# A's transposes in a fused cross-attention kernel: sixteen on VectorE, or four on TensorE

## The chip, the core and the metric

One core of a Trainium2 chip runs the whole program. The time is the device time of one execution in microseconds, the median of several runs. Its engines work side by side, each through its own list of instructions, and meet at semaphores: PE is TensorE (matmuls; PEld are its weight loads), DVE is VectorE, ACT is ScalarE, POOL is GpSimd, SP is SyncE, whose queue issues the DMAs.

## What is computed

```python
x: (16, 256, 1024)   ctx: (16, 256, 512)   W_mem: (1024, 512)   W_gate: (1024, 2048)

P      = einsum('bme,de->bmd', ctx, W_mem)          # memory_proj
S      = einsum('bnd,bmd->bnm', x, P) / sqrt(1024)
A      = softmax(S, axis=-1)
C      = einsum('bnm,bmd->bnd', A, P)               # memory_context
gate   = sigmoid(concat([x, C], -1) @ W_gate.T + b_gate)
fused  = x + gate * C
out    = fused * rsqrt(mean(fused**2, -1) + 1e-6) * norm_w
```

Everything is float32. The kernel keeps that precision with products of the type fp32r: each operand is split into a high part (a ScalarE copy that rounds) and a low part (a subtraction), and each product is made of three, high x high, high x low and low x high.

## The kernel before, in words

It works through 16 batches, one after the other: batch 0 and batch 15 are written out, batches 1 to 14 are a loop on every engine. Before batch 0 the weights are loaded, turned and split; the half of W_gate that belongs to C is multiplied with W_mem once into K, so that the gate's second half can be made from ctx: C @ G2.T = (A @ ctx) @ K.

TensorE's order within a batch, by `batch` in the tensor block:
- P from the turned ctx (`ct_h`, `ct_l`) and `wt`: 48 products of 512 columns
- the gate's X block of the second 128 rows, `gate_x(1, ...)`: 48 products of 512 columns
- the gate's X block of the first 128 rows, `gate_x(0, 0, before_s)`: the first 2 of 8 k (3 in batch 0), 6 products each
- the scores, 48 products of 256 columns, into `psum[:, 6:8, 0:M]`, the first halves of banks 6 and 7 (`s_mm`)
- the rest of the first X block, `gate_x(0, before_s, KD)`, line 803, into banks 0 and 1 (`xt_used`)
- TT, the turned A @ ctx: 24 products of 256 columns into banks 6 and 7, after the waits for `cn_ready` and `at_ready` (line 807)
- the memory products A @ P (the second after a wait for `tt_ready`), then the gate's second half.

Between scores and TT runs the softmax: DVE takes the row maxima from the score banks (line 607) and negates them (609), ACT makes `prob` in SBUF with the exponential and its row sum (450), DVE takes the reciprocal (611) and scales `prob` with it in two instructions (614, `prob_ready`). Then A has to be turned, because TT and the memory products contract over its columns: `turn_a` (lines 560 to 567) writes `at32` in SBUF with 16 VectorE transposes of 32x32 blocks and raises `at_turned`. ACT copies `at32` to `at_h` (line 457; in the trace line 400, the helper `copy`), DVE subtracts to `at_l` (line 619; in the trace line 505, the helper `low`) and raises `at_ready`. In ACT's list the copy of ctx, `ctt_h`, stands between the exponential and `at_h`. Behind `at_l` DVE has the scaling of the previous batch's last rows (547) and the turning of the next batch's x (627). POOL sets two small constants at the start (358, 359) and then subtracts some of the weights' low parts (367).

All matmuls are recorded at lines 717, 718 and 720, the three products of the helper `product`; they are told apart by the tiles they read. The order of each engine's list is written out by hand.

Of the kernel before, what the change touches and what calls it, by code (L numbers as in the profile page):

```python
# [1 line left out]

# [3 lines left out]
F32 = mybir.dt.float32  # L27
F32R = mybir.dt.float32r
ACT = mybir.ActivationFunctionType
ALU = mybir.AluOpType  # L30
AX = mybir.AxisListType

PART = 128
BLK = 32
QUADS = PART // BLK
# [4 lines left out]
def build(nc, x, ctx_in, w_mem, w_gate, b_gate, norm_w, out):  # L40
    B, N, D = x.shape
    M, E = ctx_in.shape[1:]
    NB, MB = N // PART, M // PART
    KD, KE = D // PART, E // PART
# [5 lines left out]
    with ExitStack() as ctx:  # L50
# [4 lines left out]
        def const(name, shape, dtype):  # L55
            return ctx.enter_context(nc.sbuf_tensor(name, shape, dtype))
# [5 lines left out]
        bias = const("bias", [PART, D], F32)  # L62
        norm_mem = const("norm_mem", [PART, D], F32)
        stat = const("stat", [PART, 32], F32)
        KB = 1024
        work = const("work", [PART, 68 * KB // 4], F32)

        def at(name, shape, dtype, mem, kb):

            return nc.alloc_sbuf_tensor_at(name, shape, dtype, offset=nc.lookup_mloc(mem).addr + kb * KB)  # L70

# [15 lines left out]
        prob = at("prob", [PART, NB, M], F32, work, 32)  # L87
        at_h = at("at_h", [PART, MB, N], F32R, work, 34)
        at_l = at("at_l", [PART, MB, N], F32R, work, 36)
        at32 = at("at32", [PART, MB, N], F32, work, 36)  # L90
        ctt_h = at("ctt_h", [PART, KE, MB * PART], F32R, work, 40)
        ctt_l = at("ctt_l", [PART, KE, MB * PART], F32R, work, 44)
        xrow = [at(f"xrow{i}", [PART, D], F32, work, 48 + 4 * i) for i in range(NB)]
# [16 lines left out]

        def bank(i):
            return psum[:, i, :]

# [8 lines left out]
        consts_done = sem("consts_done")  # L124
# [231 lines left out]
        @block.gpsimd  # L356
        def _(pool):
            pool.memset(minus_half, -0.5).then_inc(consts_done, 1)
            pool.memset(eps, EPS).then_inc(consts_done, 1)
            pool.wait_ge(consts_done, 2)  # L360
            for n, item in enumerate(items):
                if item in POOL_ITEMS:
                    src, high, lo = item_parts(n)
                    pool.wait_ge(item_h, n + 1)
                    if item[0] == "g1":
                        pool.wait_ge(g2_used, 8)
                    pool.tensor_tensor(lo, src, high.bitcast(F32), ALU.subtract).then_inc(item_low_pool, 1)

            def batch(b, n_blocks=NB):
                pool.wait_ge(cn_high, b + 1)  # L370
                pool.tensor_tensor(ctt_l[:, :, :].rearrange("p j (m c) -> p j m c", m=MB),
                                   stage[:, :].rearrange("p (m j c) -> p j m c", m=MB, j=KE),
                                   ctt_h[:, :, :].rearrange("p j (m c) -> p j m c", m=MB).bitcast(F32),
                                   ALU.subtract).then_inc(cn_ready, 1)
                for nb in range(n_blocks):
                    done = 2 * b + nb + 1
                    pool.wait_ge(sq_done, done)
                    pool.tensor_tensor(guarded[:, nb:nb + 1], meansq[:, nb:nb + 1], eps,  # L378
                                       ALU.add).then_inc(guarded_done, 1)
                    pool.wait_ge(guarded_done, done)  # L380
                    pool.tensor_tensor(rstd[:, nb:nb + 1], guarded[:, nb:nb + 1], minus_half,
                                       ALU.pow).then_inc(rstd_ready, 1)

            batch(0)
            with pool.Fori(1, B - 1) as b:
                batch(b)
            batch(B - 1, NB - 1)
            pool.wait_ge(sq_done, BLOCKS_BEFORE + 1)
            pool.tensor_tensor(half_sq[:, 0:1], half_sq[:, 0:1], eps, ALU.add).then_inc(guarded_done, 1)
            pool.wait_ge(guarded_done, BLOCKS_BEFORE + 1)  # L390
            pool.wait_ge(sq_done, BLOCKS_BEFORE + 2)
            pool.tensor_tensor(guarded[:, 1:2], half_sq[:, 0:1], half_sq[:, 1:2], ALU.add).then_inc(guarded_done, 1)
            pool.wait_ge(guarded_done, BLOCKS_BEFORE + 2)
            pool.tensor_tensor(rstd[:, 1:2], guarded[:, 1:2], minus_half, ALU.pow).then_inc(rstd_ready, 1)
# [3 lines left out]
        def _(act):  # L398
            def copy(dst, src):
                return nc.scalar.activation(dst, src, ACT.Copy)  # L400
# [34 lines left out]
            def batch(b, first, last):  # L435
                for t in range(4):
                    mb, j, bk = p_tile(t)
                    act.wait_ge(p_mm, 4 * b + t + 1)
                    copy(p_cols(p_h, mb, j), bank(bk)).then_inc(p_high, 1)
                    if first and t == 1:  # L440
                        for i in range(4, 8):
                            item(pos["g1", i])
                for mb, chunks in PT_PARTS:
                    act.wait_ge(p_turned, 2 * b + mb + 1)
                    copy(pt_part(pt_h, mb, chunks), pt_part(pt32, mb, chunks)).then_inc(pt_high, 1)
                if not first:
                    square(b - 1, 1)
                act.wait_ge(negmax_done, b + 1)
                for nb in range(NB):
                    nc.scalar.activation(prob[:, nb, :], psum[:, 6 + nb, 0:M], ACT.Exp, bias=negmax[:, nb:nb + 1],  # L450
                                         scale=SCALE, accum_out=rowsum[:, nb:nb + 1]).then_inc(exp_done, 1)
                act.wait_ge(s_mm, b + 1)
                act.wait_ge(cn_in, DMA * (b + 1))
                copy(ctt_h[:, :, :].rearrange("p j (m c) -> p j m c", m=MB),
                     stage[:, :].rearrange("p (m j c) -> p j m c", m=MB, j=KE)).then_inc(cn_high, 1)
                act.wait_ge(at_turned, b + 1)
                copy(at_h[:, :, :], at32[:, :, :]).then_inc(at_high, 1)
                for i in range(2):
                    act.wait_ge(tt_mm, 2 * b + i + 1)
                    copy(ctt_h[:, 2 * i:2 * i + 2, :].rearrange("p j n -> p (j n)"),  # L460
                         bank(6 + i)).then_inc(tt_high, 1)
                if not last:
                    act.wait_ge(xt_used, b + 1)
                    for nb in range(NB):
                        act.wait_ge(xs_moved, 2 * b + nb + 1)
                        copy(xt_h[:, :, PART * nb:PART * nb + PART],
                             turned[:, :].rearrange("p (k n) -> p k n", k=KD)).then_inc(xt_high, 1)
                    act.wait_ge(cs_moved, b + 1)
                    act.wait_ge(m_mm, b + 1)
                    copy(ct_h[:, :, :], turned[:, :].rearrange("p (k n) -> p k n", k=KE)).then_inc(ct_high, 1)  # L470
                for nb in range(NB - 1 if last else NB):
                    done = 2 * b + nb + 1
                    act.wait_ge(z_ready, done)

                    nc.scalar.activation(gate[:, :], gate[:, :], ACT.Tanh, scale=0.5).then_inc(tanh_done, 1)
                    if nb == 0:
                        square(b, 0)
# [25 lines left out]
        def _(dve):  # L503
            def low(dst, src, high):
                return nc.vector.tensor_tensor(dst, src, high.bitcast(F32), ALU.subtract)  # L505
# [51 lines left out]
                                                   tile[BLK * qm:BLK * qm + BLK, :, q, :])  # L557
                last.then_inc(p_turned, 1)

            def turn_a():  # L560

                for qn in range(QUADS):
                    for q in range(QUADS):
                        last = nc.vector.transpose(  # L564
                            at32.rearrange("p m (n q c) -> p n m q c", q=QUADS, c=BLK)[BLK * q:BLK * q + BLK, :, :, qn, :],
                            prob.rearrange("p n (m q c) -> p n m q c", q=QUADS, c=BLK)[BLK * qn:BLK * qn + BLK, :, :, q, :])
                last.then_inc(at_turned, 1)

            def add_rows(b, nb):
                dve.wait_ge(gm_ready, 2 * b + nb + 1)  # L570
                dve.wait_ge(xrow_in[nb], DMA * (b + 1))
# [14 lines left out]
            def batch(b, first, last):  # L586
# [26 lines left out]
                for nb in range(NB):  # L613
                    nc.vector.tensor_scalar(prob[:, nb, :], prob[:, nb, :], rowinv[:, nb:nb + 1], None,  # L614
                                            ALU.mult).then_inc(prob_ready, 1)
                dve.wait_ge(prob_ready, 2 * b + 2)
                turn_a()
                dve.wait_ge(at_high, b + 1)
                low(at_l[:, :, :], at32[:, :, :], at_h[:, :, :]).then_inc(at_ready, 1)
                if not first:  # L620
                    scale_rows(b - 1, 1)

# [57 lines left out]
            nb = NB - 1  # L680
# [29 lines left out]
        def _(pe):  # L710
# [10 lines left out]
                return last  # L721


            for g in range(4):
                if g >= 2:
                    pe.wait_ge(k_ready, g - 1)
# [18 lines left out]
            def batch(b, first, last_batch):  # L745
# [54 lines left out]
                                       [((xt_h[:, k, rows], xt_l[:, k, rows]), [(pt_h[:, k, :], pt_l[:, k, :])])],  # L800
                                       start=k == 0, stop=k == KD - 1)
                last[0].then_inc(s_mm, 1)
                gate_x(0, before_s, KD).then_inc(xt_used, 1)


                pe.wait_ge(cn_ready, b + 1)
                pe.wait_ge(at_ready, b + 1)
# [62 lines left out]
```

## Time and profile before

| | |
|---|---|
| time, median of 3 runs | 1047.63 us (1046.73 to 1047.76) |
| span of the profiled execution | 1045.4 us |
| PE busy | 1001.6 us, 96%, 4992 products |
| PEld busy | 837.6 us, 80% |
| DVE busy | 763.8 us, 73% |
| ACT busy | 281.4 us, 27% |
| POOL busy | 89.7 us, 9% |
| mean granted TensorE clock | 0.992 |

The span reaches from the first to the last instruction of the profiled execution; the measured time has a little around it. Products are pipelined: a row's duration (0.40 us for 512 columns) is longer than the distance to the next one, so the pace of TensorE is read from starts. A duration behind "x2" is that of two together. Busy shares say which engine is full over the whole; what one stage costs is read from the timeline of that stage. The bracket at the end of a row gives the idle time of the engine before it and who ended it.

### The profile page before, as it was taken

How to read it: one execution, taken by the hardware profiler on the slowest of the kernel's cores; microseconds unless marked ns; L12 is line 12 of the kernel's file. 1: busy time of each engine (PE TensorE's matmuls, PEld its weight loads, DVE VectorE, ACT ScalarE, POOL GpSimd, SP SyncE). 2: the span in 40 equal slices, each digit the busy share in tenths (PEclk: the TensorE clock that was granted, in tenths of full speed). 3: DMA queues.
4: the chain of work that ended last, by engine and by line, in shares of the span. 5: the costliest groups of instructions: out<-in, count | busy, mean ns of one | idle time of the engine just before them, and what ended most of it. 6: DMA issues, size and time to landing. Idle time of an engine off the chain costs nothing.

```text
span 1045.4 us, 13484 instructions
## 1 busy us (share of the span) xinstructions
PE 1001.6 (96%) x4992; PEld 837.6 (80%) x4992; DVE 763.8 (73%) x1277; ACT 281.4 (27%) x418; POOL 89.7 (9%) x97
## 2 busy tenths in 40 slices
PE   6997999999999999999999999999999999999996
PEld 5986788888878888887878888887888888788885
DVE  4996686776778677677768767676867767787774
ACT  4441223222221322223222222223232132222222
POOL 2240001010100101010010101000010100001010
PEclk9998999999999999999999999999999999999998
DMA  7961113112021312202131221212122131213101
GB/s 210 244 183 28 61 41 101 60 61 100 20 80 60 100 60 76 84 21 80 62 98 60 80 80 36 85 59 82 60 82 79 40 102 39 80 60 100 61 10 72
DMA packets 72895, 80.97 MB, mean 77 GB/s; under 512 B 5936, under 2 KB 59184, under 8 KB 72880
## 3 DMA queue, kind: packets, MB, share of 16 engines
q1 hardware_dynamic: 72880, 80.76, 25.1%
q8 instruction: 10, 0.16, 0.1%
q14 instruction: 5, 0.04, 0.0%
HBM read 63.96 MB, written 16.78 MB: 77 GB/s over the span
## 4 chain that ended last, share of the span: by engine, by line
PE 80%; DVE 14%; ACT 3%; issue 2%; SPq 1%; DMA 0%; POOL 0%; DVEq 0%; POOLq 0%; ACTq 0%
PE psum L717 27%; PE psum L718 26%; PE psum L720 26%; DVE at L564 7%; DVE pt L556 1%; DVE at_l L505 1%; ACT prob L450 1%; DVE stat L607 1%; ACT at_h L400 1%; DVE prob L614 1%; DVE g_l L505 0%; ACT g_h L400 0%; DMA ring<-in_L_xattn_W_gate 0%; SPq L195 0%; SPq L200 0%
## 5 line engine op out<-in xcount | busy, mean ns | idle before, releaser
L556 DVE STREAM_TRANSPOSE pt<-psum 32x256 f32<-32x256 f32 x512 | 228.2, 446 | 45.5 <-ACT p_h L400 38.8
L717 PE MATMUL psum<-g_h,xt_h 128*128 128x512 f32 x512 | 202.2, 395 | 0.9 <-DVE p_l L505 0.9
L718 PE MATMUL psum<-g_l,xt_h 128*128 128x512 f32 x512 | 202.1, 395 | 0.0
L720 PE MATMUL psum<-g_h,xt_l 128*128 128x512 f32 x512 | 160.6, 395 | 0.0
L717 PEld LDWEIGHTS psum<-g_h,xt_h 128*128 128x128 f32 x512 | 96.5, 188 | 23.1 <-DVE p_l L505 1.3
L720 PEld LDWEIGHTS psum<-g_h,xt_l 128*128 128x128 f32 x512 | 96.5, 188 | 22.7
L718 PEld LDWEIGHTS psum<-g_l,xt_h 128*128 128x128 f32 x512 | 96.6, 189 | 21.7
L717 PE MATMUL psum<-wt_h,ct_h 128*128 128x512 f32 x256 | 101.2, 395 | 0.0
L717 PE MATMUL psum<-k_h,ctt_h 128*128 128x512 f32 x256 | 100.9, 394 | 0.0
L718 PE MATMUL psum<-wt_l,ct_h 128*128 128x512 f32 x256 | 100.9, 394 | 0.0
L718 PE MATMUL psum<-k_l,ctt_h 128*128 128x512 f32 x256 | 100.9, 394 | 0.0
L400 ACT ACTIVATE pt_h<-pt 128x512 fp32r<-128x512 f32 (+1 forms) x48 | 35.4, 770 | 175.6 <-DVE pt L556 175.6
L720 PE MATMUL psum<-k_h,ctt_l 128*128 128x512 f32 x256 | 80.9, 394 | 0.0
L717 PE MATMUL psum<-pt_h,xt_h 128*128 128x256 f32 x256 | 75.3, 294 | 5.3 <-DVE pt_l L505 5.3
L564 DVE STREAM_TRANSPOSE at<-prob 32x128 f32<-32x128 f32 x256 | 77.5, 303 | 3.8
L720 PE MATMUL psum<-wt_h,ct_l 128*128 128x512 f32 x256 | 80.2, 394 | 0.0
L378 POOL TENSOR_TENSOR stat<-stat 128x1 f32<-128x1 f32 x31 | 5.9, 189 | 809.3 <-ACT turned L432 809.3
L718 PE MATMUL psum<-pt_l,xt_h 128*128 128x256 f32 x256 | 73.6, 287 | 0.0
L720 PE MATMUL psum<-pt_h,xt_l 128*128 128x256 f32 x256 | 73.5, 287 | 0.0
L400 ACT ACTIVATE p_h<-psum 128x512 fp32r<-128x512 f32 x64 | 34.7, 595 | 117.8 <-PE psum L720 117.8
L663 DVE TENSOR_TENSOR gate<-psum,bias 128x1024 f32<-128x1024 f32 x31 | 38.0, 1225 | 35.0 <-PE psum L720 35.0
L717 PEld LDWEIGHTS psum<-pt_h,xt_h 128*128 128x128 f32 x256 | 50.2, 196 | 10.6 <-DVE pt_l L505 10.2
(103 smaller groups left out, 1715.3 us busy)
## 6 DMA issues: line engine op xcount, KB each, us to landing
xrow<-in_x SPq DMA_DIRECT2D x32, 512.0 KB, 3.7
out<-xrow SPq DMA_DIRECT2D x31, 512.0 KB, 2.6
stage<-in_x SPq DMA_DIRECT2D x64, 128.0 KB, 2.8
stage<-in_ctx SPq DMA_DIRECT2D x16, 512.0 KB, 3.4
gate<-in_x SPq DMA_DIRECT2D x60, 128.0 KB, 2.7
gate<-in_ctx SPq DMA_DIRECT2D x60, 128.0 KB, 2.6
ring<-in_L_xattn_W_gate SPq DMA_DIRECT2D x44, 128.0 KB, 3.5
ring<-in_L_xattn_W_mem SPq DMA_DIRECT2D x28, 128.0 KB, 3.5
```

What stands on the lines that cost most here:

```text
L378: pool.tensor_tensor(guarded[:, nb:nb + 1], meansq[:, nb:nb + 1], eps, ALU.add).then_inc(guarded_done, 1)
L400: return nc.scalar.activation(dst, src, ACT.Copy)
L450: nc.scalar.activation(prob[:, nb, :], psum[:, 6 + nb, 0:M], ACT.Exp, bias=negmax[:, nb:nb + 1], scale=SCALE, accum_out=rowsum[:, nb:nb + ...
L505: return nc.vector.tensor_tensor(dst, src, high.bitcast(F32), ALU.subtract)
L556: last = nc.vector.transpose(pt32[BLK * q:BLK * q + BLK, :, col:col + BLK], tile[BLK * qm:BLK * qm + BLK, :, q, :])
L564: last = nc.vector.transpose(at32.rearrange("p m (n q c) -> p n m q c", q=QUADS, c=BLK)[BLK * q:BLK * q + BLK, :, :, qn, :], prob.rearrang ...
L607: nc.vector.tensor_reduce(rowmax, psum[:, 6:8, 0:M], AX.X, ALU.max).then_inc(max_done, 1)
L614: nc.vector.tensor_scalar(prob[:, nb, :], prob[:, nb, :], rowinv[:, nb:nb + 1], None, ALU.mult).then_inc(prob_ready, 1)
L663: nc.vector.tensor_tensor(gate[:, :], psum[:, 2 * nb:2 * nb + 2, :].rearrange("p h c -> p (h c)"), bias[:, :], ALU.add).then_inc(z_ready, 1)
L717: nc.tensor.matmul(tile, ah, mh, start=start and i == 0, stop=False)
L718: nc.tensor.matmul(tile, ah, ml, start=False, stop=False)
L720: last[t] = nc.tensor.matmul(tile, al, mh, start=False, stop=stop and i == len(pairs) - 1)
```

## The change

`turn_a` and `at32` go. TensorE turns A itself with four transposes of 128x128 fp32 each, `prob` against an identity matrix, into the second halves of banks 6 and 7, `psum[:, 6:8, M:2 * M]`, which the scores leave free. They stand in its list between k = 5 and k = 6 of the first X block, behind a new wait for `prob_ready`, and the last one raises `at_turned`. ACT's `at_h` and DVE's `at_l` now read that view of PSUM. POOL makes the identity at the start, in SBUF of its own, with a memset and a select, and TensorE waits for it before its first product. The source of the identity lies where `xt_h` will be later.

```diff
--- before.py
+++ after.py
...
@@ -62,6 +41,7 @@
         bias = const("bias", [PART, D], F32)
         norm_mem = const("norm_mem", [PART, D], F32)
         stat = const("stat", [PART, 32], F32)
+        ident = const("ident", [PART, PART], F32)
         KB = 1024
         work = const("work", [PART, 68 * KB // 4], F32)
 
@@ -87,7 +67,7 @@
         prob = at("prob", [PART, NB, M], F32, work, 32)
         at_h = at("at_h", [PART, MB, N], F32R, work, 34)
         at_l = at("at_l", [PART, MB, N], F32R, work, 36)
-        at32 = at("at32", [PART, MB, N], F32, work, 36)
+        ident_mem = at("ident_src", [PART, PART], F32, work, 0)
         ctt_h = at("ctt_h", [PART, KE, MB * PART], F32R, work, 40)
         ctt_l = at("ctt_l", [PART, KE, MB * PART], F32R, work, 44)
         xrow = [at(f"xrow{i}", [PART, D], F32, work, 48 + 4 * i) for i in range(NB)]
@@ -110,6 +90,9 @@
 
         def bank(i):
             return psum[:, i, :]
+
+
+        turned_probs = psum[:, 6:8, M:2 * M]
 
 
 
@@ -357,7 +340,11 @@
         def _(pool):
             pool.memset(minus_half, -0.5).then_inc(consts_done, 1)
             pool.memset(eps, EPS).then_inc(consts_done, 1)
-            pool.wait_ge(consts_done, 2)
+            pool.memset(ident_mem[:, :], 1.0).then_inc(consts_done, 1)
+            pool.wait_ge(consts_done, 3)
+            pool.affine_select(ident[:, :], ident_mem[:, :], [[-1, PART]], ALU.is_equal, 0.0, base=0,
+                               channel_multiplier=1).then_inc(consts_done, 1)
+            pool.wait_ge(consts_done, 4)
             for n, item in enumerate(items):
                 if item in POOL_ITEMS:
                     src, high, lo = item_parts(n)
@@ -454,7 +441,7 @@
                 copy(ctt_h[:, :, :].rearrange("p j (m c) -> p j m c", m=MB),
                      stage[:, :].rearrange("p (m j c) -> p j m c", m=MB, j=KE)).then_inc(cn_high, 1)
                 act.wait_ge(at_turned, b + 1)
-                copy(at_h[:, :, :], at32[:, :, :]).then_inc(at_high, 1)
+                copy(at_h[:, :, :], turned_probs).then_inc(at_high, 1)
                 for i in range(2):
                     act.wait_ge(tt_mm, 2 * b + i + 1)
                     copy(ctt_h[:, 2 * i:2 * i + 2, :].rearrange("p j n -> p (j n)"),
@@ -556,15 +543,6 @@
                         last = nc.vector.transpose(pt32[BLK * q:BLK * q + BLK, :, col:col + BLK],
                                                    tile[BLK * qm:BLK * qm + BLK, :, q, :])
                 last.then_inc(p_turned, 1)
-
-            def turn_a():
-
-                for qn in range(QUADS):
-                    for q in range(QUADS):
-                        last = nc.vector.transpose(
-                            at32.rearrange("p m (n q c) -> p n m q c", q=QUADS, c=BLK)[BLK * q:BLK * q + BLK, :, :, qn, :],
-                            prob.rearrange("p n (m q c) -> p n m q c", q=QUADS, c=BLK)[BLK * qn:BLK * qn + BLK, :, :, q, :])
-                last.then_inc(at_turned, 1)
 
             def add_rows(b, nb):
                 dve.wait_ge(gm_ready, 2 * b + nb + 1)
@@ -613,10 +591,8 @@
                 for nb in range(NB):
                     nc.vector.tensor_scalar(prob[:, nb, :], prob[:, nb, :], rowinv[:, nb:nb + 1], None,
                                             ALU.mult).then_inc(prob_ready, 1)
-                dve.wait_ge(prob_ready, 2 * b + 2)
-                turn_a()
                 dve.wait_ge(at_high, b + 1)
-                low(at_l[:, :, :], at32[:, :, :], at_h[:, :, :]).then_inc(at_ready, 1)
+                low(at_l[:, :, :], turned_probs, at_h[:, :, :]).then_inc(at_ready, 1)
                 if not first:
                     scale_rows(b - 1, 1)
 
@@ -721,6 +697,7 @@
                 return last
 
 
+            pe.wait_ge(consts_done, 4)
             for g in range(4):
                 if g >= 2:
                     pe.wait_ge(k_ready, g - 1)
@@ -800,8 +777,15 @@
                                        [((xt_h[:, k, rows], xt_l[:, k, rows]), [(pt_h[:, k, :], pt_l[:, k, :])])],
                                        start=k == 0, stop=k == KD - 1)
                 last[0].then_inc(s_mm, 1)
-                gate_x(0, before_s, KD).then_inc(xt_used, 1)
-
+                gate_x(0, before_s, 6)
+
+                pe.wait_ge(prob_ready, 2 * b + 2)
+                for mb in range(MB):
+                    for nb in range(NB):
+                        turn = nc.tensor.transpose(psum[:, 6 + mb, M + PART * nb:M + PART * nb + PART],
+                                                   prob[:, nb, PART * mb:PART * mb + PART], ident[:, :])
+                turn.then_inc(at_turned, 1)
+                gate_x(0, 6, KD).then_inc(xt_used, 1)
 
                 pe.wait_ge(cn_ready, b + 1)
                 pe.wait_ge(at_ready, b + 1)
```

## Rows read from the trace of the kernel before

**Rows 1.** Page, part 1: busy time, share of the span, instructions.
```profile
PE 1001.6 (96%) x4992; PEld 837.6 (80%) x4992; DVE 763.8 (73%) x1277; ACT 281.4 (27%) x418; POOL 89.7 (9%) x97
```

**Rows 2.** Page, part 4: chain that ended last, shares of the span by line.
```profile
PE psum L717 27%; PE psum L718 26%; PE psum L720 26%; DVE at L564 7%; DVE pt L556 1%; DVE at_l L505 1%; ACT prob L450 1%; DVE stat L607 1%; ACT at_h L400 1%; DVE prob L614 1%; DVE g_l L505 0%; ACT g_h L400 0%; DMA ring<-in_L_xattn_W_gate 0%; SPq L195 0%; SPq L200 0%
```

**Rows 3.** Windows: from:to; us, busy PE, PEld, DVE, ACT, POOL; clock, DMA share, GB/s.
```profile
106.60:109.20 2.60, 0.16 (x1) 0.00 (x0) 1.86 (x6) 0.63 (x1) 0.00 (x0) 1.00 0.64 191
...
110.50:113.70 3.20, 3.20 (x17) 3.18 (x16) 0.69 (x1) 0.71 (x2) 0.00 (x0) 0.53 0.47 133
...
518.10:578.50 60.40, 59.31 (x290) 49.15 (x289) 44.71 (x78) 15.67 (x24) 3.89 (x5) 1.00 0.22 69
...
532.30:533.50 1.20, 0.16 (x1) 0.00 (x0) 0.80 (x2) 0.37 (x1) 0.00 (x0) 1.00 0.73 156
```

**Rows 4.** Waits: who waited for whom, us in total, times, longest us.
```profile
PE psum L717 <- DVE at_l L505: 18.8, 16, 2.5
```

**Rows 5.** Timeline, TensorE, 518 to 534: start us, us, engine, line, what, tiles, shapes, count.
```profile
518.07 0.39 PE L717 MATMUL psum<-pt_h,xt_h 128*128 128x256 f32 x1
...
523.92 0.39 PE L717 MATMUL psum<-g_h,xt_h 128*128 128x512 f32 x1
...
529.51 0.40 PE L717 MATMUL psum<-g_h,xt_h 128*128 128x512 f32 x1
...
531.83 0.63 PE L720 MATMUL psum<-g_h,xt_l 128*128 128x512 f32 x2
533.54 0.36 PE L717 MATMUL psum<-at_h,ctt_h 128*128 128x256 f32 x1 [1.09 <-DVE at_l L505]
```

**Rows 6.** Timeline, VectorE and ScalarE beside it, 526 to 533.
```profile
526.31 0.62 DVE L614 TENSOR_SCALAR prob<-prob,stat 128x256 f32<-128x256 f32 x2
...
526.96 5.05 DVE L564 STREAM_TRANSPOSE at<-prob 32x128 f32<-32x128 f32 x16
...
532.04 0.63 ACT L400 ACTIVATE at_h<-at 128x512 fp32r<-128x512 f32 x1 [5.01 <-DVE at L564]
...
532.71 0.69 DVE L505 TENSOR_TENSOR at_l<-at,at_h 128x512 fp32r<-128x512 f32 x1 [0.70 <-ACT at_h L400]
```

**Rows 7.** Timeline, TensorE and VectorE in batch 0, 102 to 113.
```profile
102.02 0.62 DVE L614 TENSOR_SCALAR prob<-prob,stat 128x256 f32<-128x256 f32 x2
...
103.82 0.39 PE L717 MATMUL psum<-g_h,xt_h 128*128 128x512 f32 x1
...
106.14 0.62 PE L720 MATMUL psum<-g_h,xt_l 128*128 128x512 f32 x2
109.25 0.36 PE L717 MATMUL psum<-at_h,ctt_h 128*128 128x256 f32 x1 [2.49 <-DVE at_l L505]
...
113.34 0.63 PE L717 MATMUL psum<-p_h,at_h 128*128 128x512 f32 x1
```

**Rows 8.** Groups by line: what, shapes, count, busy us, mean ns, idle before.
```profile
L718 PE MATMUL psum<-pt_l,xt_h 128*128 128x256 f32 x256 | 73.6, 287 | 0.0
...
L718 PEld LDWEIGHTS psum<-pt_l,xt_h 128*128 128x128 f32 x256 | 50.3, 196 | 0.0
...
L505 DVE TENSOR_TENSOR p_l<-psum,p_h 128x512 fp32r<-128x512 f32 x64 | 41.2, 686 | 1.0
...
L400 ACT ACTIVATE p_h<-psum 128x512 fp32r<-128x512 f32 x64 | 34.7, 595 | 117.8 <-PE psum L720 117.8
```

**Rows 9.** Timeline, TensorE and VectorE behind TT, 536 to 540.
```profile
536.49 0.40 PE L717 MATMUL psum<-p_h,at_h 128*128 128x512 f32 x1
...
537.32 0.69 DVE L505 TENSOR_TENSOR ctt_l<-psum,ctt_h 128x512 fp32r<-128x512 f32 x1 [0.75 <-ACT ctt_h L400]
...
539.33 0.40 PE L717 MATMUL psum<-p_h,at_h 128*128 128x512 f32 x1
```

**Rows 10.** Timeline at the start, TensorE and GpSimd.
```profile
8.86 0.58 PE L717 MATMUL psum<-g_h,wn_h 128*128 128x256 f32 x1 [8.86 <-DVE wn_l L505]
...
15.06 2.42 POOL L367 TENSOR_TENSOR wn_l<-stage,wn_h 128x1024 fp32r<-128x1024 f32 x1 [14.19 <-ACT wn_h L400]
```

## The prediction

> **What bounds the kernel now.** I read the busy shares first: TensorE is busy 96% of the span [rows 1], so the question is only where its few idle stretches lie and what ends them. The chain that ended last names VectorE's transposes of A (line 564) with 7% of the span [rows 2]. That is the number that misleads: a chain follows the waits backwards, and here it runs through VectorE while TensorE has work of its own beside it. The stretches tell what it is worth. One whole batch of the steady loop takes 60.40 us, TensorE busy 59.31 of them; the missing 1.09 us lie in one place, 532.3 to 533.5 [rows 3]. The waits say who ended that place: TensorE's first product of TT waited for `at_l`, 16 times, 18.8 us in all, 2.5 us the longest [rows 4]. So batches 1 to 15 each lose the same piece, and batch 0 a longer one.
>
> In the order of time [rows 5, 6]: the 48 score products start at 518.07; the rest of the gate's X block (36 products for k = 2 to 7) starts at 523.92, its 35th at 531.83, so they come every 7.91 / 34 = 0.233 us. The last two of them end their slots at 531.83 + 0.47 = 532.30, and TT starts at 533.54: **1.24 us** in which TensorE issues nothing. Beside this VectorE has the normalized probabilities ready at 526.31 + 0.62 = 526.93, then turns A in 5.05 us (16 instructions), ScalarE copies its high part at 532.04, VectorE cuts the low part at 532.71, and TT starts at 533.54. The turn is 5.05 us long and only 1.24 us of that chain stand out behind the matmuls.
>
> In batch 0 the last pair of X products starts at 106.14 and TT at 109.25, which is 3.11 - 0.47 = **2.64 us** of nothing [rows 7] (`before_s` is 3 there, one k less to cover the chain). The granted clock was 1.00 up to then and fell to 0.53 in the stretch from 110.5 to 113.7, so TensorE was at its 1.2 GHz level for nearly all of it, after standing still [rows 3]. TT of batch 0 took 113.34 - 109.25 = 4.09 us against 536.49 - 533.54 = 2.95 us in the steady loop [rows 5, 7, 9]: another **1.14 us** that hang on the gap.
>
> **Removed.** The 16 VectorE transposes leave the path. What this can give at most is what TensorE stands still: 15 x 1.24 + 2.64 + 1.14 = 18.6 + 3.8 = **22.4 us**, not the 77 us of busy time that the line has.
>
> **Added on TensorE.** Four fp32 transposes per batch, each a 128-column weight load and a pass of 128 columns, between k = 5 and k = 6 of the X block. TensorE is the bound, so their whole time T is on the path, 16 times. No row shows a transpose on TensorE; the bounds are these. Nearest in shape are the score products: the same weight load, 256 columns, and 5.85 us / 48 = 0.122 us from start to start [rows 5]. Half of that each, if the columns alone count and the load hides, gives T = 0.24. A gain is excluded, since they are additional instructions on the bound engine. At the other end, each transpose done as four passes of that pace costs 16 x 0.122 = 1.95. I take 4 x 0.122 = 0.49, because a load of the same 128 columns hides at that pace 48 times per batch, and once the 0.20 us of an uncovered weight load [rows 8], for the change of kind of work and the wait before it: **T = 0.69**, nearer the lower end because it is nearer to the score row.
>
> **Does TensorE wait anywhere new?** Its wait on `prob_ready` stands in front of two more k, the TT block and everything behind it. It is met long before in the steady loop: k = 6 starts at 529.51 and the probabilities are there at 526.93, 2.6 us earlier [rows 5, 6]. In batch 0 it is 103.82 against 102.02 + 0.62 = 102.64, 1.2 us earlier [rows 7]. What is late next is `at_ready`. From the end of the turn to TT it was 533.54 - 532.04 = 1.50 us (ScalarE copy, VectorE subtraction, the handing over) [rows 5, 6]. Reading a score bank instead of SBUF changes little: ScalarE's copy of 128x512 from PSUM takes 595 ns and VectorE's subtraction from PSUM 686 ns [rows 8], against 0.63 and 0.69 us now. The cover behind the turn is k = 6 and 7, 12 x 0.233 = 2.79 us. So 1.29 us of margin, the wait costs nothing, and the whole bubble goes, in batch 0 too, whose cover behind the turn is the same. If that cover were gone, 1.5 us per batch would show.
>
> **The rest at nothing.** VectorE's next steps (scaling the old rows, turning X) come some 1.7 us earlier, into time in which it was idle or waiting; the stores and loads that SP's queue issues on them come earlier as well, and no wait of TensorE in the loop is for one of them. The copies of TT keep their place behind TT: VectorE's second cut of TT starts at 537.32 and is over at 538.01, needed at 539.33 by the second memory product [rows 9], 1.3 us of margin that moves along with TT. `xt_used` comes T later than the score block before, but ScalarE's copy that waits for it is queued behind the copies of TT. POOL gets a memset of 128x128 and one select at the start: its first real work starts at 15.06 after 14.19 us idle, and TensorE's first product, which now also waits for the identity, starts at 8.86 [rows 10]; even 5 us would hide.
>
> **The sum.** 22.4 - 16 x 0.69 = 22.4 - 11.0 = 11.4 us. The profiled execution has a span of 1045.4 us, which lies 2.2 below the median 1047.63 of three runs; I take the 2.2 as lying around the span and unchanged: 1045.4 - 11.4 = 1034.0 in the span, **1036.2 us** as the time, 1.1% faster. The lower bound of T gives 22.4 - 3.8 = 18.6, that is 1029.0. Breakeven is T = 22.4 / 16 = 1.40 us, 0.35 us per transpose. About 0.2% (2.1 us) is what a measurement of this kernel can tell from no change; T has to be below 1.27 for that.
>
> **Where the Trainium skill speaks against it.** The Trainium skill, TensorE: Matmul & The Clock Gate, section "Part 4: PE-mode transpose", reports about 275 ns for one transpose inside a kernel, and says transposes don't count as busy time for the clock; no row here shows either. By its 275 ns, if they didn't overlap, T would be an estimated 1.10 and the time 1042.8. The same page's Terms call transpose mode four times faster for fp32, which no run here shows and which speaks against the four passes.
>
> **Rivals.**
> A, the forecast: the transposes stream at about the pace of the score products, 1029 to 1040 (T from 0.24 to 0.93). Chance 0.69.
> B, they don't overlap: each stands alone for the 287 ns that one product of 256 columns lasts [rows 8]. T = 1.15, gain 22.4 - 18.4 = 4.0, time **1043.6**. For it: a different kind of instruction may drain the array before and after. Against it: loads are drawn ahead of running products everywhere in this trace. Chance 0.13.
> C, **slower**: an fp32 transpose costs four passes with a load each, as a full-precision fp32 product would where this kernel uses the reduced fp32r. T = 1.95, 16 x 1.95 = 31.2, minus 22.4 gives +8.8: **1056.4**. It decides from T = 1.40 upward. For it: prob is plain fp32, and every row of this trace is of fp32r products. Against it: a transpose only moves values. The Trainium skill, FP8 and Floating Point Precision, section "TensorE Precision Notes", gives four passes for true fp32. Chance 0.09.
> D, the clock: TensorE's granted clock falls behind the transposes as it fell in batch 0 behind the 2.64 us gap, and TT runs at the lower level: 16 x 1.14 = 18.2 on top of the forecast, 1054.4. Against it: the clock stayed at 1.00 through and behind the 1.24 us gap [rows 3], and 0.69 us without products is less. Chance 0.03.
> E, no difference: the turn takes the time of the bubble (T from 1.27 to 1.5), or the gain returns as a wait further on (at `tt_ready`, with 1.3 us of margin, or at `at_ready`). 1047.6. Chance 0.06.
>
> **Range and chances.** The forecast's case and B together hold 0.82; the range goes from 1030 (a little inside T = 0.24) to 1044.5 (just past B). Faster by over 0.2%: A and B, 0.82. Within: 0.06. Slower: C and D, 0.12.
>
> **What would show it.** Per batch, the start-to-start time from the last product of k = 5 to the first of k = 6 should be 0.23 + 0.69; the period of the loop 60.40 - 1.24 + 0.69 = 59.85 us; no wait of TensorE for `at_l`, in batch 0 neither; the granted clock 1.00 behind batch 0's TT; VectorE idle in place of 5.05 us of line 564. `at_l` should be ready about 1.3 us before k = 7 ends. The prediction is wrong if four transposes take over 1.3 us together, or if TensorE still stands still ahead of TT.

## The result, and the profile after

The changed kernel takes **1030.07 us** (1029.58 to 1030.12), the kernel before 1047.2 in the runs beside it: a ratio of 0.9837, with a 95% interval from 0.9823 to 0.9851. That is 17.1 us faster where 11.4 were forecast. The profiled execution has a span of 1028.0 us against 1045.4.

The waits of TensorE come first (who waited for whom, us in total, times, longest), to be held against [rows 4]. These two are its largest in the batches; in the whole list there is no line in which TensorE waits for `at_l`. The lines have moved: the three products of `product` are at 693, 694 and 696 now, the copy at 387, the subtraction at 492.

```profile
PEld psum L693 <- DVE pt_l L492: 10.3, 15, 5.7
...
PE psum L693 <- DVE pt_l L492: 5.3, 1, 5.3
```

The chain that ended last (page, part 4) has changed with it. Line 564 stood there with 7% [rows 2]; what has its place is line 785, the transposes on TensorE, with 1%:

```profile
PE psum L693 31%; PE psum L694 31%; PE psum L696 31%; DVE pt L543 1%; PE psum L785 1%; DVE g_l L492 0%; DMA ring<-in_L_xattn_W_gate 0%; ACT g_h L387 0%; SPq L178 0%; SPq L183 0%; POOL wn_l L354 0%; DVE pt_l L492 0%; DVE xrow L670 0%; DVE stage L666 0%; ACT turned L479 0%
```

The windows for one batch (us, busy PE, PEld, DVE, ACT, POOL, clock, DMA share, GB/s), where [rows 3] had 59.31 busy of 60.40: now all of 59.50 is busy. VectorE's share fell from 44.71 to 39.86 us and bought nothing by itself (run 4 below). The second row is the microsecond with the transposes in it, the third the stretch in batch 0 from the transposes to the memory products: the clock is 1.00 in all, also where it had been 0.53.

```profile
508.60:568.10 59.50, 59.50 (x293) 49.61 (x292) 39.86 (x63) 15.64 (x24) 3.89 (x5) 1.00 0.21 71
...
520.00:521.00 1.00, 1.00 (x9) 0.82 (x7) 0.00 (x0) 0.27 (x1) 0.10 (x1) 1.00 0.00 0
...
103.40:109.60 6.20, 6.20 (x43) 5.58 (x41) 2.46 (x3) 1.20 (x2) 1.47 (x1) 1.00 0.49 129
```

The timeline of TensorE around the transposes, as [rows 5]:

```profile
519.63 0.63 PE L696 MATMUL psum<-g_h,xt_l 128*128 128x512 f32 x2
520.10 0.60 PE L785 MATMUL psum<-ident,prob 128*128 128x128 f32 x4
520.45 0.48 PE L693 MATMUL psum<-g_h,xt_h 128*128 128x512 f32 x1
520.77 0.40 PE L694 MATMUL psum<-g_l,xt_h 128*128 128x512 f32 x1
...
522.87 0.62 PE L696 MATMUL psum<-g_h,xt_l 128*128 128x512 f32 x2
523.33 0.28 PE L693 MATMUL psum<-at_h,ctt_h 128*128 128x256 f32 x1
523.44 0.28 PE L694 MATMUL psum<-at_l,ctt_h 128*128 128x256 f32 x1
...
526.20 0.40 PE L693 MATMUL psum<-p_h,at_h 128*128 128x512 f32 x1
```

From the first transpose to the second X product behind them it is 520.77 - 520.10 = 0.67 us, where one slot of 0.23 would have been: **T = 0.44 us**, 0.11 per transpose. The first X product behind them, 0.32 us from its row to the next, takes part of it. TT follows the X block without a gap. Beside it ScalarE and VectorE, as [rows 6]:

```profile
520.73 0.60 ACT L387 ACTIVATE at_h<-psum 128x512 fp32r<-128x512 f32 x1 [3.11 <-PE psum L785]
...
521.36 0.69 DVE L492 TENSOR_TENSOR at_l<-psum,at_h 128x512 fp32r<-128x512 f32 x1 [3.85 <-ACT at_h L387]
```

`at_l` ends at 522.05, 1.28 us before TT's first row, and VectorE sits idle for 3.85 us where it turned A.

**Where the 17.4 us of the two spans come from.** The first product of P marks the start of a batch. Batch 1 and batch 15 of the changed kernel start here:

```profile
126.42 0.40 PE L693 MATMUL psum<-wt_h,ct_h 128*128 128x512 f32 x1
...
959.62 0.40 PE L693 MATMUL psum<-wt_h,ct_h 128*128 128x512 f32 x1
```

and at 130.52 and 976.10 in the timeline of the kernel before. So 14 batches took 833.20 in place of 845.58, 59.51 us each in place of 60.40: 12.4 us. Batch 15 to the end is 0.9 shorter (69.3 to 68.4). Batch 0 is 4.3 shorter (72.5 to 68.3), and it starts 0.2 later (58.00 to 58.16). Together 12.4 + 0.9 + 4.3 - 0.2 = 17.4.

### The profile page after: what moved, and what is told of

Read it like the earlier page. It is cut to its first block, busy times and chain, and to the rows that moved or that the text cites. A ratio compares the mean times of both kernels' runs of the same rounds, so it can differ in the third digit from the quotient of the medians.

```text
span 1028.0 us, 13360 instructions
## 1 busy us (share of the span) xinstructions
PE 1003.3 (98%) x5056; PEld 843.8 (82%) x5056; DVE 686.4 (67%) x1021; ACT 280.8 (27%) x418; POOL 90.1 (9%) x99
## 4 chain that ended last, share of the span: by engine, by line
PE 94%; DVE 3%; ACT 1%; SPq 1%; DMA 0%; issue 0%; POOL 0%; DVEq 0%; POOLq 0%; ACTq 0%
PE psum L693 31%; PE psum L694 31%; PE psum L696 31%; DVE pt L543 1%; PE psum L785 1%; DVE g_l L492 0%; DMA ring<-in_L_xattn_W_gate 0%; ACT g_h L387 0%; SPq L178 0%; SPq L183 0%; POOL wn_l L354 0%; DVE pt_l L492 0%; DVE xrow L670 0%; DVE stage L666 0%; ACT turned L479 0%
## 5 line engine op out<-in xcount | busy, mean ns | idle before, releaser
L419 ACT ACTIVATE turned<-xrow 128x1024 f32<-128x1024 f32 x31 | 32.9, 1060 | 91.4 <-DVE xrow L550 91.4
```

Of the source, the lines that this page charges most:

```text
L419: nc.scalar.activation(turned[:, :], xrow[nb][:, :], ACT.Square, scale=SCALE, accum_out=meansq[:, nb:nb + 1]).then_inc(sq_done, 1)
```

## The experiments

All are variants of the changed kernel unless said otherwise. "Period" is the mean time from batch to batch, from batch 1 to 15, read from each timeline in the way shown above. "To before" is the ratio to the runs of the kernel before that were made beside that variant (medians from 1047.04 to 1047.2).

| run | time, us | to before | period, us |
|---|---|---|---|
| before | 1047.2 | 1 | 60.40 |
| changed | 1030.07 | 0.9837 | 59.51 |
| 1 transposes twice | 1037.18 | 0.9904 | 59.94 |
| 2 ordinary fp32 products | 1038.05 | 0.9914 | 59.97 |
| 3 no cover | 1057.78 | 1.0103 | 61.25 |
| 3b one k of cover | 1035.66 | 0.9893 | 59.86 |
| 4 VectorE's turn beside it | 1031.10 | 0.9849 | 59.52 |
| 5 before, more cover | 1046.66 | 0.9994 | 60.46 |
| 6 no turn | 1023.56 | 0.9770 | 59.07 |
| 7 half on each engine | 1027.66 | 0.9814 | 59.30 |
| 8 batch 0 ordered anew | 1027.76 | 0.9811 | 59.52 |
| 9 runs 7 and 8 together | 1024.24 | 0.9784 | 59.30 |

**Runs 1 and 6: what T is made of.** Run 1 issues the transposes twice, run 6 not at all.

```diff
-                for mb in range(MB):
+                for mb in (0, 1, 0, 1):
                     for nb in range(NB):
                         turn = nc.tensor.transpose(...)
```

> The four transposes are issued twice, eight per batch. In the changed kernel four of them put off the X products behind them by 0.44 us. Theory 1 (they stream, each costs its slot of 0.109 us and nothing is paid for going in and out): 4 x 0.109 x 16 = 7.0 us more than the changed kernel, 1037.0 us. Theory 2 (part of the 0.44 is paid once, for the change of kind of work, as the 0.20 us of the forecast was): 0.24 x 16 = 3.8 us more, 1033.9 us.

```diff
-                gate_x(0, before_s, 6)
+                gate_x(0, before_s, 6).then_inc(at_turned, 1)
-                pe.wait_ge(prob_ready, 2 * b + 2)
-                for mb in range(MB):
...
-                turn.then_inc(at_turned, 1)
...
-        turned_probs = psum[:, 6:8, M:2 * M]
+        turned_probs = psum[:, 6:8, 0:M]
```

> Leaves the turning of A out: ScalarE and VectorE split the raw score halves of the banks instead, at the same times. It measures T by its absence. Theory 1 (T = 0.44 us per batch, all of it on the path): 16 x 0.44 = 7.1 us less than the changed kernel, 1023.0 us, period 59.08 us. Theory 2 (something else than the transposes sets the pace there, so nothing or more is gained): 1030 or well under 1020.

Measured: 1037.18 with eight, 1030.07 with four, 1023.56 with none, periods 59.94, 59.51 and 59.07. The first four cost 0.444 us per batch and the second four 0.429, so nothing to speak of is paid for going in and out. Theory 1 held in both, to within 0.6 us. The steady batches of run 6 have no idle time either (59.07 us busy of 59.07):

```profile
151.74:210.81 59.07, 59.07 (x289) 49.23 (x288) 39.87 (x62) 15.64 (x24) 3.88 (x5) 1.00 0.22 71
```

**Run 2: rival C.**

```diff
-                        turn = nc.tensor.transpose(psum[...], prob[...], ident[:, :])
+                        turn = nc.tensor.matmul(psum[...], prob[...], ident[:, :], start=True, stop=True)
```

> Each transpose is issued as an ordinary fp32 product with the identity. Theory 1 (transpose mode is what makes it one pass; an ordinary fp32 product takes four with their loads): T goes from 0.44 to about 16 x 0.122 = 1.95 us, 16 x 1.51 = 24 us more, 1054 us, slower than before, which is the prediction's rival C. Theory 2 (no difference between the two): 1030.1 us.

Measured: 1038.05. Neither theory held: an ordinary fp32 product costs more than a transpose, but twice as much, not four times. The two views of the tile `prob` show why (minimum, median and maximum duration in ns; first and last start; shapes). First the changed kernel, then run 2:

```profile
L785 PEld LDWEIGHTS psum<-ident,prob x64: 138/140/144, 103.3 to 996.5; 128*128 128x128 f32 x64
L785 PE MATMUL psum<-ident,prob x64: 270/272/273, 103.5 to 996.6; 128*128 128x128 f32 x64
```

```profile
L785 PEld LDWEIGHTS psum<-ident,prob x128: 188/192/192, 103.9 to 1004.4; 128*128 128x128 f32 x128
L785 PE MATMUL psum<-ident,prob x128: 271/275/275, 104.1 to 1004.5; 128*128 128x128 f32 x128
```

The 64 ordinary products are 128 records, two each, at about the pace of the transposes:

```profile
164.09 1.05 PE L785 MATMUL psum<-ident,prob 128*128 128x128 f32 x8
164.90 0.48 PE L693 MATMUL psum<-g_h,xt_h 128*128 128x512 f32 x1
```

T doubles with the records: the period is 59.97 - 59.51 = 0.46 us longer, against the 0.44 that the transposes cost. The whole is (1038.05 - 1030.07) / 16 = 0.50 more per batch; the rest of it lies in batch 0, which is 0.9 us longer here, 0.4 of them in its score block, which stands ahead of the edit. Even so the change would have been faster than before. The trace shows two records per product and twice the cost of a transpose. Whether a record is one pass through the array or more, it doesn't show.

**Runs 3 and 3b: the cover.** The transposes stand behind k = 7 (the diff), and in run 3b behind k = 6, with 7 in place of both 6.

```diff
-                gate_x(0, before_s, 6)
+                gate_x(0, before_s, KD).then_inc(xt_used, 1)
...
-                gate_x(0, 6, KD).then_inc(xt_used, 1)
```

> The four transposes stand behind the whole first X block, so nothing covers ScalarE's copy and VectorE's subtraction. Theory 1 (position is what the gain rests on): 1.5 us of gap plus 0.1 for starting again show per batch, 16 x 1.6 = 26 us more than the changed kernel, 1056 us, slower than before. Theory 2 (the shorter chain alone pays): stays below 1047. The clock should stay at 1.00, since the 1.24 us gap of before left it there.

Measured: 1057.78, slower than before, with a gap of 1.50 us that `at_l` ends in all 16 batches (24.1 us of waits in all):

```profile
534.82 0.60 PE L785 MATMUL psum<-ident,prob 128*128 128x128 f32 x4
536.92 0.36 PE L693 MATMUL psum<-at_h,ctt_h 128*128 128x256 f32 x1 [1.50 <-DVE at_l L492]
```

The clock stayed at 1.00 in the gap and behind it, in batch 0 too, as expected (windows: us, busy PE, PEld, DVE, ACT, POOL, clock, DMA share, GB/s):

```profile
534.80:537.00 2.20, 0.70 (x6) 0.46 (x4) 0.91 (x2) 0.60 (x1) 0.00 (x0) 1.00 0.37 91
536.90:541.00 4.10, 4.08 (x29) 3.91 (x30) 3.21 (x4) 1.52 (x3) 0.00 (x0) 1.00 0.41 155
```

Theory 1 held, 1.8 us above its 1056, since the gap from start to start is 2.10 - 4 x 0.11 = 1.66 us and not 1.5: moved by two k, the same edit turns from 1.6% faster to 1.0% slower.

> The four transposes stand between k = 6 and k = 7, so one k (6 products, 1.40 us) covers the copies. Without any cover TT started 1.77 us after the last transpose did; with one k TensorE is through 0.14 + 1.40 + 0.08 = 1.62 us after it. Theory 1 (the chain behind the turn takes 1.77 us and the margin of the changed kernel is 1.25 us): 0.15 us of gap and 0.08 for starting again per batch, 16 x 0.2 = 3.5 us more than the changed kernel, 1033.5 us. Theory 2 (the chain gets longer or shorter with X products beside it): clearly another value, 1030 if shorter.

Measured: 1035.66, 5.6 us more and not 3.5. The chain is what theory 1 says; my sum of the cover was wrong:

```profile
164.49 0.60 PE L785 MATMUL psum<-ident,prob 128*128 128x128 f32 x4
164.84 0.48 PE L693 MATMUL psum<-g_h,xt_h 128*128 128x512 f32 x1
...
166.60 0.35 PE L693 MATMUL psum<-at_h,ctt_h 128*128 128x256 f32 x1
```

TT starts 2.11 us after the first transpose; in run 3 it was 2.10. The chain is the same with and without X products beside it. The last of the four transposes starts at 164.49 + 3 x 0.109 = 164.82 and the first X product at 164.84, 0.02 us later and not 0.14, so the cover was overrated by 0.12: 0.12 + 0.23 = 0.35 per batch, 5.6 us. In the changed kernel 523.33 - 520.10 = 3.23 us lie between the same two rows, 1.13 more than the chain needs.

**Run 4: is VectorE's relief worth anything?** `turn_a` is back with three of its four outer steps and writes a tile of its own.

```diff
+                dve.wait_ge(prob_ready, 2 * b + 2)
+                turn_a()
                 dve.wait_ge(at_high, b + 1)
                 low(at_l[:, :, :], turned_probs, at_h[:, :, :]).then_inc(at_ready, 1)
```

> VectorE does 12 of its 16 old transposes again, into a tile that nobody reads, in the time in which it would now wait for the high part; TensorE turns A as in the changed kernel. Theory 1 (the gain is TensorE's gap alone, the 3.8 us per batch taken from VectorE are worth nothing): 1030.1 us. Theory 2 (the 6 us by which the gain went past the forecast come from VectorE having less to do): about 1034 to 1036 us.

Measured: 1031.10, 1.0 us above the changed kernel. VectorE's 3.77 us are back and the period is 59.52, as without them. `at_l` in its steady batches starts as soon as the high part is there:

```profile
518.21 3.77 DVE L552 STREAM_TRANSPOSE at<-prob 32x128 f32<-32x128 f32 x12
522.02 0.69 DVE L493 TENSOR_TENSOR at_l<-psum,at_h 128x512 fp32r<-128x512 f32 x1
```

The profiled spans differ by 0.7 us, and that lies ahead of batch 1: batch 0 is 0.55 us longer. There three k stand between the scores and the transposes in place of four, so the transposes that nobody reads hold `at_l` up (it ends at 107.14, TT starts at 107.28), and the last X products and TT take 0.3 us more together. The other 0.25 us are in the score block, ahead of the edit. Theory 2 is out.

**Run 5: could more cover have done it without the change?** This is the kernel before with `before_s` 2 and 1.

```diff
-                before_s = 3 if first else 2
+                before_s = 2 if first else 1
```

> The kernel before with one k of the first X block moved from ahead of the scores to behind them (before_s 2 and 1 in place of 3 and 2), so that seven k cover the softmax and VectorE's turn. Theory 1 (the gap only moves: the scores wait for the turned P, whose wait was met with nothing to spare): TensorE waits 1.4 us ahead of the scores in place of 1.24 behind the X block, 1047 to 1050 us. Theory 2 (more cover is free): all gaps go, 1047.6 - 22 = 1025 us, better than the change.

Measured: 1046.66, ratio 0.9994 (0.9984 to 1.0004): no difference. The gap moved, as theory 1 says. The wait for `at_l` is gone from the loop (one of 1.1 us is left, in batch 0) and the scores wait for the turned P:

```profile
PE psum L717 <- DVE pt_l L505: 26.0, 16, 6.7
```

```profile
514.29 0.63 PE L720 MATMUL psum<-g_h,xt_l 128*128 128x512 f32 x2
516.19 0.38 PE L717 MATMUL psum<-pt_h,xt_h 128*128 128x256 f32 x1 [1.28 <-DVE pt_l L505]
```

In both kernels the scores start 14.00 us after the first X product of the batch (504.07 to 518.07 before, 502.19 to 516.19 here): the turned P sets that, and a k taken away ahead of the scores leaves a hole of its own length there. So in the loop another division of these eight k gives nothing; a shorter chain does. That the total is still the same comes of two opposite parts: the 15 steady batches are 0.06 us longer each, and batch 0 is 2.1 us shorter (70.38 against 72.51). There too the gap only moved, but what is left of it ahead of TT fell from 2.64 to 1.2 us, the clock was 1.00 from 97.5 to 112, and TT and the memory products are 1.5 us shorter; the other 0.6 us are the score block, which varies by more than that (run 8).

**Run 7: turn half of A on each engine.** TensorE makes two transposes after k = 4. VectorE turns the other half (`turn_a` for mb = 0, into `at32`) in 16 transposes of 64 columns meanwhile, and copy and subtraction are split in two.

```diff
-                for mb in range(MB):
+                for mb in (1,):
...
+                dve.wait_ge(prob_ready, 2 * b + 2)
+                turn_a()
...
+                low(at_l[:, 1, :], bank(7)[:, M:2 * M], at_h[:, 1, :])
...
+                low(at_l[:, 0, :], at32[:, :], at_h[:, 0, :])
```

> TensorE turns only the second half of A (two transposes, one k earlier), VectorE turns the first half in 16 transposes of 64 columns in its idle time. Theory 1 (VectorE's part is free as long as it ends before the X block does): T halves, 16 x 0.22 = 3.5 us less than the changed kernel, 1026.6 us. Theory 2 (16 small transposes and the split copies take too long, at_l comes late and the gap is back): 1030 us or more.

Measured: 1027.66, period 59.30, which is 0.213 below the changed kernel's: half of T. Theory 1 held in the loop (15 x 0.213 = 3.2 us); the time fell by 2.4, with single runs from 1027.0 to 1028.7. Batch 0 is no shorter (68.40 us): with one k less behind the scores, the transposes wait 0.3 us for `prob` there and TT 0.4 us for `at_l`. VectorE's transposes take 235 ns each with 64 columns against 303 with 128, 3.98 us for all 16, and `at_l` is ready at 521.37, in front of TT at 522.04:

```profile
516.49 3.98 DVE L554 STREAM_TRANSPOSE at<-prob 32x64 f32<-32x64 f32 x16
...
520.95 0.42 DVE L496 TENSOR_TENSOR at_l<-at,at_h 128x256 fp32r<-128x256 f32 x1
```

**Run 8: batch 0.**

```diff
-                before_s = 3 if first else 2
+                before_s = 5 if first else 2
+                after_s = 7 if first else 6
...
-                gate_x(0, before_s, 6)
+                gate_x(0, before_s, after_s)
...
-                gate_x(0, 6, KD).then_inc(xt_used, 1)
+                gate_x(0, after_s, KD).then_inc(xt_used, 1)
```

> Batch 0 alone is ordered anew: five k of the first X block ahead of the scores in place of three, where TensorE stands still for 5.3 us and its clock falls, two k ahead of the transposes and one behind. Theory 1: 2 x 1.39 = 2.8 us of that wait are filled, the clock falls for a shorter time (1 to 2 us of the score block), less 0.3 us for the thinner cover of softmax and of the copies: 1026 us. Theory 2 (the two k are filled into a wait but come back as waits behind the scores): 1029 to 1030 us.

Measured: 1027.76, between the theories. Batch 0 takes 65.96 us against 68.26, 2.3 us less. 0.6 of them are the score block (7.33 against 7.95 us), whose clock was a little higher (0.77 against 0.70):

```profile
91.00:98.40 7.40, 7.31 (x48) 7.31 (x49) 1.93 (x4) 0.00 (x0) 0.00 (x0) 0.77 0.00 0
```

That it is the edit that did this isn't shown, since the score block of batch 0 varies by up to 1.1 us between kernels that are the same up to there (7.25 in run 3, 8.37 in run 2). The other 1.7 us are what is left of the 2.8 that were filled. The waits show the filled gap, and new ones:

```profile
PE psum L693 <- DVE pt_l L492: 2.5, 1, 2.5
...
PEld psum L693 <- POOL ctt_l L358: 0.9, 1, 0.9
```

It stood still 2.5 us in place of 5.3 ahead of the scores. The transposes (line 786 here) now wait for `prob`, which VectorE has ready at 101.43:

```profile
100.76 0.63 PE L696 MATMUL psum<-g_h,xt_l 128*128 128x512 f32 x2
101.48 0.66 PE L786 MATMUL psum<-ident,prob 128*128 128x128 f32 x4
101.89 0.48 PE L693 MATMUL psum<-g_h,xt_h 128*128 128x512 f32 x1
```

TT then waits for POOL's `ctt_l`, the low part of ctx that POOL cuts in each batch, and not for `at_l`: with the cover cut to one k, that is next.

**Run 9: the two together**, with all of A turned on TensorE in batch 0 alone.

> Puts the two gains together: batches 1 to 15 turn half of A on TensorE and half on VectorE, as in the run with the half, and batch 0 has the new order with all of A turned on TensorE. Theory 1 (they are independent, one per place): period 59.30 us as with the half, 0.213 x 15 = 3.2 us, and batch 0 shorter by 2.3 us: 1030.1 - 5.5 = 1024.6 us. Theory 2 (they share a cause, so only one counts): 1027 us.

Measured: 1024.24 (1023.36 to 1025.55), ratio 0.9784 (0.9770 to 0.9797), the period of run 7 and the batch 0 of run 8 (65.99 us). The two gains are independent and add up; it is the fastest of all that turn A, 5.8 us below the change. The reserve about the score block of batch 0 (7.35 us here) holds for this run too.

## Why the prediction came out as it did

Direction, mechanism and place were right. The gain was half as large again as forecast, 17.1 us and not 11.4, two thirds of the difference because the term T was too large. 1030.07 lies at the very edge of the range, and one of its four runs (1029.58) outside it: that the range held is in part luck.

- **What bounds**: right. The chain's 7% for line 564 were not the gain; TensorE's standstill was, and it is gone in all 16 batches. Runs 3, 3b and 5 move it and get it back.
- **The cost T**: this term failed. 0.69 us was put in, 0.44 measured (0.444 and 0.429 for the first and second four, runs 6 and 1), which makes 16 x 0.25 = 4.0 us of the missing 6.0 (17.4 in the span and not 11.4). Of its two parts 4 x 0.122 was nearly right (4 x 0.109). The added uncovered weight load of 0.20 us does not exist: the wait in front was met 2.6 us earlier (517.52 against 520.10), and the first load starts at 519.86, beside the X products, as others do. Where the wait was met last, in batch 0 of runs 7, 8 and 9, the transposes up to the next product take 0.06 to 0.07 us more (0.41 in place of 0.35 in run 8), so even there the term would not have been 0.20.
- **The gap's price**: 1.24 us of nothing were put in; a gap also costs 0.08 behind it. TT takes 2.95 us after a standstill [rows 5, 9] and 526.20 - 523.33 = 2.87 without one. The difference lies in its first product: from 533.54 it was 0.20 us to the next one, and it is 0.11 now. 15 x 0.08 = 1.2 us. The row behind the one at 533.54 in the kernel before:

```profile
533.74 0.28 PE L718 MATMUL psum<-at_l,ctt_h 128*128 128x256 f32 x1
```

- **Batch 0**: the gap of 2.64 and the 1.14 of the lower clock came as forecast. What was left out are the memory products: their block took 6.03 us at first, still at the lower clock for its first two, and takes 5.68 now, 0.35 us. The score block of batch 0 was 0.46 us shorter, but it varies by more than that between kernels that are the same up to there (run 8), so it can't be credited to the change. 4.0 + 1.2 + 0.35 + 0.46 is 6.0, minus the 0.2 by which batch 0 started later: 5.8 of 6.0, in which the 0.46 may be chance.
- **The margins**: `at_ready` 1.29 us forecast, 1.13 by run 3's chain; the new wait for `prob_ready` never showed; the copies from PSUM took 0.60 and 0.69 us, as their rows said.
- **At nothing**: POOL's two instructions end at 1.42 us, ahead of TensorE's first product at 9.32. VectorE's relief is worth nothing (run 4).
- **Rival B**, transposes that don't overlap: out. Each lasts 272 ns by its record and costs 109. The Trainium skill, TensorE: Matmul & The Clock Gate, section "Part 4: PE-mode transpose", gives about 275 ns for one in a kernel. The trace agrees with it as a duration (270 to 273 ns, fp32; the page speaks of 128x128 in bf16), and it would have given 1042.8 us if it were taken for the cost.
- **Rival C**, passes of full fp32: out for transposes, T is 0.44 and not 1.95. Its price is out for ordinary products too: run 2 shows two records and twice T, 0.90 us per batch. The Trainium skill, FP8 and Floating Point Precision, section "TensorE Precision Notes", has four passes for true fp32. Run 2 shows two records per product, which neither confirms nor refutes the number of passes; that such a product costs four times a transpose is refuted here.
- **Rival D**, the clock: out, 1.00 around the transposes, and around the eight of run 1 (0.87 us per batch). The gap of 1.50 us in run 3 didn't bring it down either; the one of 2.64 in batch 0 had.
- **Rival E**: its second half, a gain that returns as a wait elsewhere, is what run 5 does in the loop; the change doesn't.

## What to carry to other kernels

A chain through a helper engine is worth only what of it stands out behind the bound engine's own work: measure that gap on the bound engine, start to start, and put what follows a gap (slow first instructions, a fallen clock) on the same bill. When work is moved onto the bound engine to shorten such a chain, its pace, not the duration of its records, is the price, and its position decides the sign: there has to be enough work behind it to cover the rest of the chain. Where the helper engine has time left, half of the work there may be free (run 7, in the loop).

## What the runs showed of the hardware that I had not expected

- A transpose of 128 columns costs 0.109 us and a score product of 256 columns 0.122: half the columns, a tenth less time. Both have a weight load of 128 columns, so the load may set the pace; no run tells that apart. In run 2 the loads are recorded as 192 ns in place of 140, and the pace is 0.11 as well (eight records in 164.90 - 164.09 = 0.81 us), so the recorded length of a load isn't its price.
- A weight load for a transpose lasts 140 ns by its record, for an ordinary product 188 to 196.
- An ordinary fp32 product of 128 columns is recorded as two weight loads and two products.
- A standstill of TensorE costs 0.07 to 0.08 us more in the first product behind it, at an unchanged clock, whether it was 0.27 us from start to start (run 3b: TT's first rows at 166.60 and 166.79), 1.24 (before) or 1.66 (run 3: 536.92 and 537.12).
